# Third attention: bias subtractions start after normalisation, key loads come first, and VectorE subtracts a quarter of every third head

## What is computed

```
x = x + L1_xattn(layernorm(x), ctx, ctx, bias, bias, pad, attn_mask)

q = (query @ Wq.T + bq).reshape(B, T, 16, 16)      # B = 4, T = S = 512
k = (key   @ Wk.T + bk).reshape(B, S, 16, 16)
scores = q k^T * 16 ** -0.5 + attn_mask            # (B, 16, 512, 512)
scores = where(pad, -inf, scores)
scores = scores + spatial_bias + directional_bias  # the same tensor twice
out = softmax(scores) @ v
return out @ Wo.T + bo
```

## Time and profile before

| what | value |
|---|---|
| median of 3 runs | 1803.09 us (1798.42 to 1805.94) |
| the profiled execution's own time | 1807.59 us |
| its span | 1805.7 us |
| busy share of the span | PE 87%, VectorE 62%, ScalarE 45%, GpSimd 26% |
| `queries` | 897.0 to 957.9 us of the span |
| third attention, from the clearing of pO | from 958.45 us |
| last subtraction of GpSimd ends | 1257.8 us |

### The profile page before, as it was taken

How to read it: one execution, slowest core, us unless ns; L and a number is a source line. 1 busy time by engine, 2 the same in 40 slices (tenths; PEclk the granted TensorE clock), 3 DMA queues, 4 the chain that set the end, 5 groups by cost and what they waited for, 6 DMA issues and landing times. The chain is left out here.

```text
span 1805.7 us, 24507 instructions
## 1 busy us (share of the span) xinstructions
PE 1570.1 (87%) x8312; PEld 1039.5 (58%) x8312; DVE 1127.4 (62%) x2783; ACT 812.5 (45%) x1301; POOL 470.5 (26%) x247
## 2 busy tenths in 40 slices
PE   6799999988999996599656898889798997999992
PEld 3566666656444454499624555555554555766671
DVE  6699999667887857266486887788524520222224
ACT  1488888621766662222146777778322221111110
POOL 0000000020000002211144998898132260111110
PEclk9999999999999998799878999999889998999996
DMA  7633433015344323667356889985160024444414
GB/s 256 239 106 94 119 96 96 23 70 175 96 118 107 90 80 130 237 225 255 131 201 223 302 305 283 277 283 203 52 229 0 0 79 151 139 147 148 145 64 152
DMA packets 139394, 276.59 MB, mean 153 GB/s; under 512 B 24080, under 2 KB 68624, under 8 KB 129808
## 3 DMA queue, kind: packets, MB, share of 16 engines
q1 hardware_dynamic: 131904, 258.98, 44.1%
q0 software_dynamic: 5264, 14.06, 2.2%
q10 hardware_dynamic: 2112, 2.10, 0.3%
HBM read 215.36 MB, written 59.69 MB: 152 GB/s over the span
## 5 line engine op out<-in xcount | busy, mean ns | idle before, releaser
L699 DVE CUSTOM_DVE_ANT_0 X<-pS,M 128x512 f32<-128x512 f32 x512 | 340.6, 690 | 60.7 <-POOL M L626 39.8
L649 PE MATMUL pT<-ident,X 128*128 128x128 f32 x2048 | 309.6, 275 | 1.4 <-ACT PT L735 1.3
L640 PE MATMUL pS<-k,q 65*128 65x512 f32 (+1 forms) x512 | 256.2, 500 | 61.8 <-DVE mx L699 36.3
L626 POOL TENSOR_TENSOR M<-C,M 128x2048 f32<-128x2048 f32 x60 | 272.9, 4580 | 54.5 <-DMA M<-in_fside_Bx16xSxS 54.4
L649 PEld LDWEIGHTS pT<-ident,X 128*128 128x128 f32 x2048 | 257.0, 141 | 42.1 <-issue 4.2
L640 PEld LDWEIGHTS pS<-k,q 65*128 65x128 f32 (+1 forms) x512 | 99.0, 193 | 180.8 <-DVE mx L699 102.9
L537 PE MATMUL pO<-PT,V 128*17 128x512 f32 x1536 | 201.2, 599 | 1.0 <-ACT OT L920 1.0
L893 DVE TENSOR_REDUCE nm<-pS 128x1 fp32r<-128x512 f32 x256 | 163.6, 686 | 39.7 <-PE pS L835 28.8
L727 ACT ACTIVATE X<-X,nm 128x512 f32<-128x512 f32 x256 | 164.0, 712 | 27.9 <-DVE nm L705 27.8
L727 ACT ACTIVATE X<-X,mx 128x512 f32<-128x512 f32 x256 | 164.9, 715 | 7.4 <-DVE mx L699 7.1
L712 DVE COPY PT<-pT 128x1024 f32<-128x1024 f32 x128 | 156.2, 1220 | 6.9 <-PE pT L649 6.9
(11 more groups left out here) (299 smaller groups left out, 2240.3 us busy)
## 6 DMA issues: line engine op xcount, KB each, us to landing
M<-in_fside_Bx16xSxS SPq DMA_DIRECT2D x64, 1024.0 KB, 7.4
w<-in_L_ffn_ew SPq DMA_DIRECT2D x48, 512.0 KB
w<-in_L_ffn_W SPq DMA_DIRECT2D x23, 1024.0 KB, 12.2
q<-q_stacks SPq DMA_DIRECT2D x192, 64.0 KB, 3.2
M<-mask SPq DMA_DIRECT2D x16, 512.0 KB, 3.6
k<-k_stacks SPq DMA_DIRECT2D x128, 64.0 KB, 3.0
xs<-top_in SPq DMA_DIRECT2D x51, 128.5 KB
k_stacks<-hi SPq DMA_DIRECT2D x24, 256.0 KB, 2.5
```

The source lines that it names most:

```text
L626: eng.tensor_tensor(M[:, slot], C[:, b % 2], M[:, slot], ALU.subtract).then_inc(s_m, 1)
L640: eng.matmul(pS[:, qt % 2, :], of, by, start=True, stop=True).then_inc(s_s, 1)
L649: ins = eng.transpose(pT[:, kt, qt * P:(qt + 1) * P], X[:, t % 3, qt, kt * P:(kt + 1) * P], self.ident[:])
L699: eng.tensor_tensor_reduce(X[:, i % 3, qt, :], pS[:, qt % 2, :], M[:, slot, qt, :], 2.0 if mask is None else 1.0, HIGHEST if mask is None ...
```

## The change

It has three parts.

1. In `queries` GpSimd waits for all 16 row tiles to be normalised (s_z) before it subtracts, and it does so for three heads instead of four (READY = 3). The fourth head's subtraction moves to GpSimd's loop in the attention.
2. `load_two` is split. In `queries` the 12 key loads of pairs 0 and 1 are issued right after the loads of M. The 4 query loads of pair 0 stay behind the stores of n = 3, those of pair 1 go behind the stores of n = 5 instead of n = 4. In the attention the pair's loads are the same, queries of both heads first, then keys.
3. In the attention, for heads i with i % 3 == 2 from 5 on (20 heads, 5 to 62), GpSimd subtracts three of the four blocks, and VectorE the last one, in an instruction of its own behind the wait for GpSimd and ahead of the four reductions. The reduction of the last block waits for it (s_own). The load of C also waits until the heads that used the slot are reduced.

```
+READY = 3
...
+            def shared_out(i):
+                return not per_group and i >= READY and i % 3 == 2
...
                     def load_common(b):
                         need(eng, s_m, H * (b - 1))
+                        need(eng, s_x, 4 * H * (b - 1))
                         eng.dma_start(C[:, b % 2], common[b]).then_inc(s_c[b % 2], 16)
...
                     if not per_group:
-                        for i in range(4, NBH):
+                        for i in range(READY, NBH):
...
                             eng.wait_ge(s_f[slot], 16 * (turn + 1))
-                            eng.tensor_tensor(M[:, slot], C[:, b % 2], M[:, slot], ALU.subtract).then_inc(s_m, 1)
+                            qts = slice(0, ST - 1 if shared_out(i) else ST)
+                            eng.tensor_tensor(M[:, slot, qts], C[:, b % 2, qts], M[:, slot, qts], ALU.subtract).then_inc(s_m, 1)
...
                                 eng.wait_ge(s_m, i + 1)
+                            if shared_out(i):
+                                b = i // H
+                                eng.wait_ge(s_c[b % 2], 16 * (b // 2 + 1))
+                                eng.wait_ge(s_f[slot], 16 * (turn + 1))
+                                eng.tensor_tensor(M[:, slot, ST - 1], C[:, b % 2, ST - 1], M[:, slot, ST - 1], ALU.subtract).then_inc(s_own, 1)
                             need(eng, s_t, 2 * (i - 2))
                             for qt in range(ST):
+                                if shared_out(i) and qt == ST - 1:
+                                    eng.wait_ge(s_own, len([h for h in range(i + 1) if shared_out(h)]))
...
                         eng.dma_start(self.M[:, n], side[n]).then_inc(self.s_f[n], 16)
+                    for pair in range(2):
+                        self.load_two_keys(eng, KS, self.k2, pair, pair, self.s_qk[pair])
                     for n in range(NQ):
...
-                        if n in (3, 4):
-                            self.load_two(eng, QS, KS, self.q2, self.k2, n - 3, n - 3, self.s_qk[n - 3])
+                        if n in (3, 5):
+                            pair = (n - 3) // 2
+                            self.load_two_queries(eng, QS, self.q2, pair, pair, self.s_qk[pair])
...
                     eng.wait_ge(s_zero, 2)
+                    eng.wait_ge(s_z, NT)
                     eng.wait_ge(self.s_c[0], 16)
-                    for n in range(4):
+                    for n in range(READY):
                         eng.wait_ge(self.s_f[n], 16)
                         eng.tensor_tensor(self.M[:, n], self.C[:, 0], self.M[:, n], ALU.subtract).then_inc(self.s_m, 1)
```

More of the change, by code:

```diff
@@ L518, in load_third, with load_two_queries, load_two_keys @@
         eng.dma_start(k[rows, slot].bitcast(F32), KS[heads][:, :, 1 - part].rearrange("h d s -> d h s")).then_inc(sem, 16)
-    def load_two(self, eng, QS, KS, q, k, slot, pair, sem):
+    def load_two_queries(self, eng, QS, q, slot, pair, sem):
+        quarter = AUX // 2
+        for j in range(2):
+            rows = QS[2 * pair + j].rearrange("d r s -> (d r) s")
+            low, high = j * AUX, j * AUX + quarter
+            eng.dma_start(q[low:low + quarter, slot, j, :].bitcast(F32), rows).then_inc(sem, 16)
+            eng.dma_start(q[high:high + quarter, slot, j, :].bitcast(F32), rows).then_inc(sem, 16)
+    def load_two_keys(self, eng, KS, k, slot, pair, sem):
         quarter = AUX // 2
@@ L524, in load_two @@
             head = 2 * pair + j
-            rows = QS[head].rearrange("d r s -> (d r) s")
             low, high = j * AUX, j * AUX + quarter
-            eng.dma_start(q[low:low + quarter, slot, j, :].bitcast(F32), rows).then_inc(sem, 16)
-            eng.dma_start(q[high:high + quarter, slot, j, :].bitcast(F32), rows).then_inc(sem, 16)
             eng.dma_start(k[low:low + quarter, slot, :].bitcast(F32), KS[head].rearrange("d r s -> (d r) s")).then_inc(sem, 16)
@@ L531, in load_two @@
                 eng.dma_start(k[high + 1 - part:high + quarter:2, slot, :].bitcast(F32), KS[head, :, part]).then_inc(sem, 16)
+    def load_two(self, eng, QS, KS, q, k, slot, pair, sem):
+        self.load_two_queries(eng, QS, q, slot, pair, sem)
+        self.load_two_keys(eng, KS, k, slot, pair, sem)
     @staticmethod
@@ L572, in attention_turned @@
             pB = self.ps("pB", [P, 512], ctx)
-            names = ("s_s", "s_x", "s_nm", "s_pad", "s_p", "s_t", "s_ea", "s_ed", "s_o", "s_oc", "s_b", "s_r", "s_n")
-            s_s, s_x, s_nm, s_pad, s_p, s_t, s_ea, s_ed, s_o, s_oc, s_b, s_r, s_n = (self.sem(n, ctx) for n in names)
+            names = ("s_s", "s_x", "s_nm", "s_pad", "s_p", "s_t", "s_ea", "s_ed", "s_o", "s_oc", "s_b", "s_r", "s_n", "s_own")
+            s_s, s_x, s_nm, s_pad, s_p, s_t, s_ea, s_ed, s_o, s_oc, s_b, s_r, s_n, s_own = (self.sem(n, ctx) for n in names)
             if mask is not None:
```

## The result

The change made the kernel slower. The median is 1835.53 us (4 runs, 1832.02 to 1838.59) against 1804.51 us for the kernel before (4 runs); the ratio is 1.0171, with a 95% interval of 1.0129 to 1.0213. The forecast was 1815 us and the range reached to 1840. The profiled execution took 1838.59 us, 31.0 more than that of before, and its span is 1836.8 us, 31.1 more. The forecast's own account (D) ran only to 1828; the measured time lies between it and the 1844 of rival (C), and inside the range because the range took in half of (C).

The account below looks back on a forecast made before the run. GpSimd's subtractions were taken to set the attention's pace, 4.83 us a head. Start -11.9 us and attention +23.5 us gave +11.6, a median near 1815 us; range 1782 to 1840.

Parts of the forecast that it names:

- (D): The forecast's own account: start -11.9 us, attention +23.5 us, median near 1815, its own range 1798 to 1828; chance 0.50.
- rival (C): In the attention, both shared quarters of every six-head cycle are blocked in full: +41 us, 1844; chance 0.18.
- The normalisation gets its 14.7 us back: In `queries`, VectorE regains 14.7 us lost beside GpSimd's subtractions, since these now come after normalisation.
- Low halves wait for GpSimd instead, start -11.9 us: In `queries`, VectorE's low halves wait out GpSimd's three subtractions; the attention starts at 946.6 against 958.45.
- A VectorE subtraction of two SBUF tensors is blocked by GpSimd's current instruction: In the attention, VectorE's quarter waits until GpSimd's current subtraction ends, a stall of up to 4.5 us.
- rival (A): In the attention, VectorE's quarter doesn't wait for GpSimd: stage -15.6 us, start -18, total 1769.5; chance 0.07.
- Rival (B), the stage stays: In the attention, quarters wait 2.2 us on average, the stage keeps its length, only the queries gain: 1791; chance 0.20.
- How many are blocked: Of the attention's twenty quarters, one blocked per six-head cycle, both in 3 of 9 cycles; ten or more stretched.
- The stage, +23.5 us: From the attention's start to GpSimd's last subtraction: 322.9 us against 299.4, from blocked quarters and 3 us for late loads.
- the head behind a stall: In the attention, VectorE's head after a blocked quarter takes 4.55 us, since PE fills only two banks ahead.
- The tail, unchanged: From the last head to the output, the time is as before.

Follow-up runs that it names:

- e3: The changed kernel with VectorE's quarter subtraction replaced by bn_stats, which reads one SBUF tensor, leaving that block unsubtracted: 1780.03 us, ratio 0.9906.
- e6: The changed kernel with VectorE's quarter formed in place in PSUM, so no instruction on it reads two SBUF tensors: 1778.24 us, ratio 0.9876.
- e8: The changed kernel, with GpSimd waiting for VectorE's quarter before the subtraction behind a shared head: 1791.72 us, ratio 0.9962 to the kernel before.
- e2: The kernel before with only the shared quarter added for the same 20 heads, queries as before: 1850.12 us, ratio 1.0277.
- e1: The changed kernel without the shared quarter, GpSimd subtracting all four blocks of every head: 1783.01 us, ratio 0.9909 to the kernel before.
- e7: The kernel before with only the new wait for all 16 normalised row tiles: 1789.19 us, ratio 0.9938.

## Why the prediction was right, and where its sizes were off

- **The normalisation gets its 14.7 us back**: right; both stretched instructions have their short length.
- **Low halves wait for GpSimd instead, start -11.9 us**: -11.1. The mechanism was right in the main: four of them took 16.67 us. I had let two low halves run back to back, as the four additions of the earlier trace rows did; but SP's stores of halves 2 and 3 went out at 928.79 and 933.97, so GpSimd got in between. That is what the Trainium skill says (SBUF — State Buffer, Who interferes with whom: the ports are kept for one instruction). The start worked out by its wording was 948; measured 947.35, between the two. That the sum came within 0.8 us is partly luck: GpSimd was done at 938.27 and not at 941.0, and the last two low halves waited for ScalarE (0.96 and 0.64 us) and not for GpSimd.
- **A VectorE subtraction of two SBUF tensors is blocked by GpSimd's current instruction**: right, and shown by e3, e6 and e8, which take away the second input or the neighbour, and by e2, which has nothing but the quarter. The rival (A), no wait, is excluded.
- **Rival (B), the stage stays**: its mean stall of 2.2 us a quarter came true, (56.0 - 13.6) / 20 = 2.1 us, and yet the stage did not stay. The stalls were not spread over GpSimd's instruction: eight were 0.1 us or none, twelve were 2.8 to 4.3. And its price, three heads at 3.87 us behind each quarter, left out the slow head that is described below.
- **How many are blocked**: the forecast had 13 up to head 59 (head 5, one in each of nine cycles, and both in three of them). It was 11, with both in one cycle only, and then head 62, which the forecast did not count. Rival (C), both in every cycle, did not come.
- **The stage, +23.5 us**: +37.3. This is the term that was mis-sized. Nine cycles of six heads were given 276.6 us and 3 for late loads; from the end of head 5's quarter (972.83) to that of head 59 (1266.26) they took 293.4, 32.6 each. The pieces before and after it came as forecast (25.5 us for 25.4, 17.7 for 17.85), so this is all of the 13.7 us that were missing. The step that failed is the head behind a stall, taken as 4.55 us from the earlier trace rows, where VectorE's wait was 2.89 us. Behind the 4.73 us quarter above it is 6.31 (1170.62 to 1176.93). PE's timeline and the windows of that stretch (length, busy us of PE, PEld, VectorE, ScalarE, GpSimd, granted clock, DMA share, GB/s) show what was left out:

```profile
1166.54 0.60 PE L666 MATMUL pT<-ident,X 128*128 128x128 f32 x4
1171.37 0.79 PE L657 MATMUL pS<-k,q 128*128 128x512 f32 x1 [4.22 <-DVE mx L723]
1171.96 1.06 PE L666 MATMUL pT<-ident,X 128*128 128x128 f32 x4
...
1174.22 1.91 PE L549 MATMUL pO<-PT,V 128*17 128x512 f32 x8
```

```profile
1162.00:1166.00 4.00, 2.99 (x21) 1.76 (x22) 3.74 (x10) 3.60 (x5) 4.00 (x3) 1.00 0.86 238
1166.00:1170.00 4.00, 1.14 (x10) 0.83 (x8) 4.00 (x2) 1.01 (x1) 4.00 (x1) 0.96 0.94 391
1170.00:1174.00 4.00, 2.63 (x10) 2.16 (x10) 3.04 (x8) 0.00 (x0) 4.00 (x2) 0.50 0.87 358
1174.00:1178.00 4.00, 4.00 (x21) 1.80 (x20) 2.58 (x6) 1.80 (x4) 4.00 (x2) 0.69 0.38 108
```

  The stall reaches PE, which idles for 4.22 us. Its granted clock then goes from full (2.4 GHz) to half (1.2 GHz) for the next stretch: four transposes take 1.06 us instead of 0.60, eight weighings 1.91 instead of 1.05, and VectorE waits for scores. So a stall costs its own length and one slow head more. The ten blocked heads from 5 to 53 took 4.84 to 6.40 us from their first reduction to the next head, 11.2 us in all above ten times 4.55. That is most of the 16.8 us by which the nine cycles exceeded their 276.6, though fewer quarters were blocked in them than forecast; what made up the rest is not separated. The part of the clock in it is read off the trace, since no run kept PE's clock up through the stalls. One stall did: behind the quarter of head 14 (1020.13, 3.89 us) the granted clock stayed at 1.00 and the head took 4.87 us, while the other heads with a weighing had 0.50 to 0.71 and took 5.34 to 6.40. From 971 to 1285 us the mean granted clock was 0.91, in e8's attention (960 to 1240) it was 0.99.
- **The tail, unchanged**: +4.9 us. Overlooked: head 62 is a shared one and meets the subtraction of head 63.
- **The sum**: +11.6 forecast, +31.0 measured. Sign and cause were right, the size was not, and the range of the forecast's own account ended 7.5 us short of the measured median.

## What to carry to other kernels

Before work is handed from GpSimd to VectorE, look at where both inputs of the new VectorE instruction live: with two in SBUF it queued here behind the subtraction that GpSimd was in, and since GpSimd set the pace, it was in one most of the time. Put one operand in PSUM (e6), or let GpSimd wait for the handed-over piece (e8). Judge such a split by the duration of the instruction and not by the waits, and price a stall that reaches PE with the slow head that follows it.

## What was not expected

- A VectorE instruction's stall is inside its duration (0.68 us becomes 4.97), so busy shares rise: VectorE was busy for 64% of a longer span, against 62%, and of the 51 us more that it was busy, 42 were stalls in the quarters.
- Who is blocked can differ between two executions of the same code. With the additions of x and y 0.03 us behind GpSimd's start, GpSimd waited 1.28 us in one profile; in e2's profile, where GpSimd had begun earlier, three additions waited 4.3 us each.
- Part of a term that I read as the kernel's own may belong to one execution. From 1110 to 1150 us the profile of before moves 261 GB/s at a DMA share of 0.99, and GpSimd waits for M five times, 7.4 us, and twice more by 1171, 3.6 us. The same stretch of e1 moves 311 GB/s at 0.95, and GpSimd's waits for M are 13.1 us in the whole stage. That is most of the 9 us by which e1's stage was shorter; why the transfers were slower in that execution is open. It is not all one execution's: by the medians e1 gains 16.3 us and e7 10.1, of which the start explains 11.1 and 6.0. Some 4 to 5 us in each come from elsewhere, and no run separates them. The windows of before, and then of e1 (columns as above):

```profile
1110.00:1150.00 40.00, 33.42 (x203) 21.50 (x202) 28.01 (x67) 25.46 (x37) 32.60 (x9) 0.87 0.99 261
```

```profile
1110.00:1150.00 40.00, 35.06 (x245) 22.41 (x245) 32.50 (x81) 29.95 (x45) 38.93 (x9) 1.00 0.95 311
```
